# Moving the second layer's first projections into the first layer's feed-forward, pairing the early maximum tiles, and taking the up product off VectorE

## The reference, cut to what matters

```python
# layer 0 feed-forward, weights of three values
hidden = silu(xn @ wu.T) * (xn @ wg.T);  out = hidden @ wd.T
# layer 1 attention, 16 heads of 16
q, k = rope(xn @ q_w.T + q_b), rope(xn @ k_w.T + k_b);  v = xn @ v_w.T + v_b
probs = softmax(q @ k.T * 0.25);  out = (probs @ v) @ out_w.T + out_b
# layer 1 feed-forward (fwht: Walsh-Hadamard transform)
h = fwht(xn * SU_ug) / 64
h = silu(h @ W_gate.T * wsg) * (h @ W_up.T * wsu)
out = (fwht(h * SU_dp) / 64) @ W_down.T * wsd
```

## Time and profile before

| | us |
|---|---|
| median of 3 runs | 798.71 (797.28 to 798.75) |
| the profiled execution | 799.5 |
| its span, first to last instruction | 797.7 |
| TensorE busy | 722.2 (91%) |
| VectorE busy | 568.9 (71%) |
| ScalarE busy | 416.1 (52%) |
| GpSimd busy | 247.7 (31%) |

### The profile page before, as it was taken

How to read it: one execution, slowest core, us unless ns; L and a number is a source line. 1 busy time by engine, 2 the same in 40 slices (tenths; PEclk the granted TensorE clock), 3 DMA queues, 4 the chain that set the end, 5 groups by cost and what they waited for, 6 DMA issues and landing times.

```text
span 797.7 us, 10977 instructions
## 1 busy us (share of the span) xinstructions
PE 722.2 (91%) x4190; PEld 446.2 (56%) x4190; DVE 568.9 (71%) x922; ACT 416.1 (52%) x547; POOL 247.7 (31%) x241
## 2 busy tenths in 40 slices
PE   3678798969697989899999999999999999999997
PEld 3467687957466878656656656533333433333344
DVE  4887666675365664898898998688888468888016
ACT  2532323345254433132122122799999899999983
POOL 0156855333224444231121021112124313412520
PEclk9988999999799999999999999999999999999999
DMA  6145101000101246443311110234444424433321
GB/s 241 54 148 185 51 0 53 1 1 1 53 1 53 80 139 208 154 154 111 106 54 54 54 49 6 70 127 153 124 146 134 140 81 134 152 115 101 114 61 54
DMA packets 25703, 74.13 MB, mean 93 GB/s; under 512 B 4604, under 2 KB 5980, under 8 KB 24692
## 3 DMA queue, kind: packets, MB, share of 16 engines
q1 hardware_dynamic: 21124, 65.37, 24.6%
q0 software_dynamic: 3808, 7.60, 3.3%
q10 hardware_dynamic: 720, 0.48, 0.2%
HBM read 54.54 MB, written 23.06 MB: 97 GB/s over the span
## 4 chain that ended last, share of the span: by engine, by line
PE 66%; DVE 16%; issue 7%; ACT 6%; POOL 2%; DMA 1%; SPq 0%; DVEq 0%; ACTq 0%; POOLq 0%
PE PS L718 20%; PE PS L959 15%; PE PS L945 11%; PE PS L724 9%; PE PS L928 6%; DVE mx L1238 4%; PE PS L918 4%; DMA stg<-in_wa 1%; ACT P L1412 1%; DVE XD L1046 1%; PE PS L798 1%; DVE sg L1177 1%; DVE sg L1169 1%; DVE XL L1053 1%; ACT sg L1378 1%
## 5 line engine op out<-in xcount | busy, mean ns | idle before, releaser
L1412 ACT ACTIVATE P<-PS 128x1024 f32<-128x1024 f32 x256 | 248.8, 1023 | 26.7 <-PE PS L945 26.3
L1245 DVE TENSOR_REDUCE mx<-PS 128x1 f32<-128x512 f32 x288 | 181.9, 682 | 31.1 <-PE PS L928 29.7
L1490 POOL TENSOR_TENSOR hl<-sg,hh 128x512 fp32r<-128x512 f32 x64 | 83.1, 1299 | 222.6 <-ACT hh L1385 222.6
L1238 DVE TENSOR_REDUCE mx<-PS 128x2 f32<-128x1024 f32 x112 | 132.2, 1218 | 15.0 <-PE PS L918 14.5
L959 PE MATMUL PS<-P,VV 128*32 128x512 f32 x1024 | 136.4, 605 | 0.1
L945 PE MATMUL PS<-QS,KS 64*128 64x512 f32 x512 | 116.1, 457 | 1.2 <-ACT P L1412 0.9
L945 PEld LDWEIGHTS PS<-QS,KS 64*128 64x128 f32 x512 | 48.1, 183 | 122.9 <-ACT P L1412 112.3
L1385 ACT ACTIVATE hh<-sg 128x512 fp32r<-128x512 f32 x64 | 40.4, 631 | 135.6 <-DVE sg L1180 83.9
L928 PE MATMUL PS<-KM,QM 64*128 64x512 f32 x288 | 77.5, 396 | 0.0
L1380 ACT ACTIVATE sg<-PS,cols 128x512 f32<-128x512 f32 x32 | 22.0, 689 | 82.7 <-PE PS L718 82.7
L918 PE MATMUL PS<-KM,QM 64*128 64x512 f32 x224 | 51.5, 484 | 9.7 <-DVE mx L1238 7.1
(11 more groups left out here) (199 smaller groups left out, 1353.0 us busy)
## 6 DMA issues: line engine op xcount, KB each, us to landing
QM<-scr_q SPq DMA_DIRECT2D x16, 512.0 KB, 4.4
KM<-scr_k SPq DMA_DIRECT2D x16, 512.0 KB, 5.4
QS<-scr_q SPq DMA_DIRECT2D x16, 512.0 KB, 4.4
KS<-scr_k SPq DMA_DIRECT2D x16, 512.0 KB, 5.3
scr_q<-spl SPq DMA_DIRECT2D x24, 256.0 KB, 3.4
scr_k<-spl SPq DMA_DIRECT2D x24, 256.0 KB, 3.1
scr_o<-OE POOLq DMA_DIRECT2D x14, 256.0 KB, 2.6
stg<-in_tern SPq DMA_DIRECT2D x3, 1024.0 KB, 4.8
```

The lines of the kernel that those rows point to most:

```text
L1238: e.tensor_reduce(mx[p % 2][:, :, qt, half], PS[:, b:b + 2, :], AX.X, ALU.max).then_inc(q["mx"], 2)
L1245: e.tensor_reduce(mx[p % 2][:, h, qt, half:half + 1], bank[b], AX.X, ALU.max).then_inc(q["mx"], 1)
L1412: e.activation(P[s % 4][:, half * 1024:(half + 1) * 1024], PS[:, b:b + 2, :].rearrange("p b n -> p (b n)"), ACT.Exp).then_inc(q["ex"], 1)
L1490: e.tensor_tensor(hl[f % 4][:, :], sg[f % 3][:, :], r32(hh[f % 4][:, :]), ALU.subtract).then_inc(q["hl"], 1)
```

## The change

- Four of the eight projections (chunks 0 and 1, queries and keys) with their rotations, splits and writes move into the end of `side0`. Their rotation and split buffers are a set of their own (`rots[0]`, `spls[0]`), in the space of the weights' staging. The tables `COS` and `SIN` load at the start of layer 0's last chunk in the list, and need only the norms of chunks 0 and 1 done; chunk 2 and 3's norms get another buffer. `load_m(0)` and `load_m(1)` are put before the end of layer 0.
- `RATE0` goes from 0.8 to 0.9; what is left of `side0` is no longer emptied before layer 1 but runs on in front of `side1`.
- Early tiles are put in twos (`two`), and beside the last projections each two comes with a value block. The rates are 0.9 for the first 32 steps and then 0.64 twos a step (before: 1.15 for 22 steps, then 1.62 tiles a step). `EARLY` goes from 112 to 106. The row of maxima takes a bank of `pf`, one tile later.
- In layer 1 the up block is read out of PSUM by ScalarE (`us = up * wsu`), the product `sg * us` is done by GpSimd, and the high part (`hidden`) follows behind the next gate in ScalarE's queue, the low part with it on GpSimd. `us` lies in the same space as `hh`. The up block's bank is free after ScalarE's copy.

```diff
-EARLY, MOST = 112, 3
+EARLY, MOST = 106, 3
 
 PROJECT = (56, 112, 120)
 FIRST = 12
-RATE0 = 0.8
-RATE1 = 1.15
-RATE2 = 1.62
+RATE0 = 0.9
+RATE1 = 0.9
+RATE2 = 0.64
...
         for m in range(8):
             bg = pf.next()
             put("gate", layer, c, m, bg)
+            if layer and m:
+                put("hidden", c, m - 1)
             yield
             put("up", layer, c, m, pf.next())
             yield
...
         for m in (5, 6, 7):
             put("down", layer, c, m)
+            if layer and m == 5:
+                put("hidden", c, 7)
             yield
         put("ffn_end", layer, c)
...
+    def qk(c, n, between, count):
+        put("qk", c, n, ps.next(), ps.next())
+        yield
+        for _ in range(count):
+            between()
+            yield
+        put("qk_split", c, n)
...
+        for c in (0, 1):
+            for n in range(2):
+                yield from qk(c, n, lambda: None, 4)
+        put("load_m", 0)
+        put("load_m", 1)
...
+                if (layer, c, k) == (0, 3, 0):
                     put("load_cs")
...
-    for _ in sd0:
-        pass
...
-            if u == 2 and p > 0:
-                rows(p - 1, ring)
+            if u == 3 and p > 0:
+                rows(p - 1, pf)
...
-        def qk(c, n, between, count):
-            put("qk", c, n, ps.next(), ps.next())
-            yield
-            for _ in range(count):
-                between()
-                yield
-            put("qk_split", c, n)
-
         def v():
-            put("v", next(tts), ps.next())
-
-        def early():
+            tt = next(tts, None)
+            if tt is not None:
+                put("v", tt, ps.next())
+
+        def two():
             tile(ps)
-
+            tile(ps)
+
+        def two_and_v():
+            two()
+            v()
+
+        yield
+        yield
         for i in range(4):
             put("ones_v", i)
-        for c in (0, 1):
-            for n in range(2):
-                yield from qk(c, n, v, 3)
-        put("load_m", 0)
-        put("load_m", 1)
+        yield
         yield from qk(2, 0, v, 4)
-        yield from qk(2, 1, early, 4)
+        yield from qk(2, 1, two_and_v, 4)
         for n in range(2):
-            yield from qk(3, n, early, 5)
+            yield from qk(3, n, two_and_v, 4)
         while len([o for o in order if o[0] == "max"]) < EARLY:
-            early()
+            two()
             yield
 
-    sd1 = side1()
+    sd1 = chain(sd0, side1())
     main1 = main(1)
-    weave(islice(main1, 22), sd1, RATE1)
+    weave(islice(main1, 32), sd1, RATE1)
     weave(main1, sd1, RATE2)
     for _ in sd1:
         pass
...
+        us = [sb(f"us{i}", (156, 158, 160, 76)[i], [128, 512]) for i in range(4)]
...
-        XD = [sb(f"XD{i}", 16 + 4 * i, [128, 4, 256]) for i in range(2)]
+        XD = [sb(f"XD{i}", (16, 20, 198)[i], [128, 4, 256]) for i in range(3)]
...
-        rot = [sb(f"rot{i}", 84 + 2 * i, [128, 512]) for i in range(4)]
-        spl = [sb(f"spl{i}", 92 + 2 * i, [128, 512], F32R) for i in range(4)]
+        rots = [[sb(f"rot{b}{i}", (190, 84)[b] + 2 * i, [128, 512]) for i in range(4)] for b in range(2)]
+        spls = [[sb(f"spl{b}{i}", (174, 92)[b] + 2 * i, [128, 512], F32R) for i in range(4)] for b in range(2)]
...
-                e.wait_ge(q["lnb"], 14)
+                e.wait_ge(q["lnb"], 12)
...
             def load_m(p):
                 if p == 0:
-                    e.wait_ge(q["lnl"], 16)
+                    e.wait_ge(q["d"], 32)
                     e.wait_ge(d["pad"], 32)
...
                     e.wait_ge(q["bx"], 8)
+                    e.wait_ge(q["lnl"], 16)
...
                 sums(bank[b], wide(TG, None, m * 128, c) if layer == 0 else wide(UGH, UGL, m * 128, c)).then_inc(q["u"], 1)
-                freed[b] = q["h"], f + 1
+                freed[b] = (q["h"], f + 1) if layer == 0 else (q["ue"], f - 31)
...
-                if n == 6:
-                    e.wait_ge(q["lnb"], 10)
                 if n == 7:
-                    e.wait_ge(q["pd"], 4)
+                    e.wait_ge(q["lnb"], 14)
...
             def up(layer, c, m, b):
-                f = 32 * layer + 8 * c + m
+                if layer:
+                    return
+                f = 8 * c + m
                 s = sg[f % 3]
                 e.wait_ge(q["u"], f + 1)
-                if layer == 0:
-                    e.wait_ge(q["v1"], f + 1)
-                    e.tensor_tensor(s[:, :], s[:, :], bank[b], ALU.mult).then_inc(q["h"], 1)
-                else:
-                    e.wait_ge(q["t"], f + 1)
-                    e.scalar_tensor_tensor(s[:, :], bank[b], col("wsu", m), s[:, :], ALU.mult, ALU.mult).then_inc(q["h"], 1)
+                e.wait_ge(q["v1"], f + 1)
+                e.tensor_tensor(s[:, :], s[:, :], bank[b], ALU.mult).then_inc(q["h"], 1)
...
                 if i == 0:
                     e.wait_ge(d["cs"], 32)
+                    e.wait_ge(q["pd"], 4)
+                if i == 4:
                     e.wait_ge(q["d"], 32)
...
             def up(layer, c, m, b):
                 f = 32 * layer + 8 * c + m
+                if layer == 0:
+                    e.wait_ge(q["h"], f + 1)
+                    e.activation(hh[f % 4][:, :], sg[f % 3][:, :], ACT.Copy).then_inc(q["hh"], 1)
+                else:
+                    e.wait_ge(q["u"], f + 1)
+                    e.activation(us[f % 4][:, :], bank[b], ACT.Copy, scale=col("wsu", m)).then_inc(q["ue"], 1)
+
+            def hidden(c, m):
+                f = 32 + 8 * c + m
                 e.wait_ge(q["h"], f + 1)
                 e.activation(hh[f % 4][:, :], sg[f % 3][:, :], ACT.Copy).then_inc(q["hh"], 1)
...
+                    if i == 0:
+                        e.wait_ge(q["pu"], 4)
+                    else:
                         e.wait_ge(d[f"sp{2 * m}"], 32 * i)
...
+            def low_part(f):
+                e.wait_ge(q["hh"], f + 1)
+                e.tensor_tensor(hl[f % 4][:, :], sg[f % 3][:, :], r32(hh[f % 4][:, :]), ALU.subtract).then_inc(q["hl"], 1)
+
             def up(layer, c, m, b):
                 f = 32 * layer + 8 * c + m
-                e.wait_ge(q["hh"], f + 1)
-                e.tensor_tensor(hl[f % 4][:, :], sg[f % 3][:, :], r32(hh[f % 4][:, :]), ALU.subtract).then_inc(q["hl"], 1)
+                if layer == 0:
+                    low_part(f)
+                else:
+                    s = sg[f % 3]
+                    e.wait_ge(q["ue"], f - 31)
+                    e.tensor_tensor(s[:, :], s[:, :], us[f % 4][:, :], ALU.mult).then_inc(q["h"], 1)
+
+            def hidden(c, m):
+                low_part(32 + 8 * c + m)
...
+                    for j in range(4):
+                        e.wait_ge(d[f"sp{j}"], (128, 64)[j % 2])
```

15 lines of the change are left out of this document (9 added, 6 removed).

## The result

The changed kernel takes 812.19 us (median of 4 runs, 811.05 to 812.99) against 798.73 for the kernel before (4 runs): a ratio of 1.0171, 95% interval 1.0154 to 1.0189. I had predicted 786. The profiled execution of after took 811.97 us, its span is 810.2.

A forecast was written before the change was run, and what follows sets the result against it. It took VectorE as the bound in layer two's chunks 1 to 3 and TensorE in the last stage. Terms -19.3 - 0.8 + 6 + 0.7 = -13.4 against 799.5 gave 786.1, said as 786, range 775 to 797.

The forecast's parts named there:

- Chunks 1 to 3: Layer two's later chunks: fewer tiles, all in twos, and a relieved VectorE take 153.0 us for 172.3, -19.3.
- The up chain: Layer two's copy, product, high and low part: 4.3 us, hidden in a 6.4 us period, cost 0 to 0.5.
- Layer two's first chunk: Fewer projections and value blocks but more tiles: 75.0 us for 75.8, -0.8, bounds -6 and +5.
- 14 value blocks, 20 tiles in twos, 64.7: Layer two's first chunk: TensorE's work after the change, with 4 projections, 64.7 us, before waits of 11.3 less 1.
- Layer one: Four projections add 11.1 us, 6 of the stall and half clock go, packing adds 1: +6, bounds 0 and +18.
- the attention is packed denser, +1: Layer one: 0.9 side pieces for 0.8 beside the feed-forward cost 1 us.
- So 39.5: Layer one's last chunk: 31.9 us of TensorE work plus waits of 2.5, 2.7 and 2.3; before it took 39.2.
- Last stage: Exponentials and remaining maxima: six tiles become 12 more halves, filling four steps, +0.7 us.
- Slower than before: Rival: each projection moved into layer one exposes rotation and split, +34 there, -20 in layer two: 812; chance 0.07.
- The first layer pays: Rival: VectorE bounds layer one's last chunk, waits double, half clock follows, +14 for +6: 794; chance 0.13.
- The bursts are absorbed: Rival: waits of 3 in layer two's chunks 1 to 3, layer one's stall gone, +1 there: 776; chance 0.15.
- It does not do what it says: Rival: the up chain sets layer two's pace and TensorE waits for low parts: no change, 799; chance 0.05.

The follow-up runs named there:

- before_up: The kernel before with only layer two's up product moved, as a copy on ScalarE and a product on GpSimd: 803.5 us.
- vfirst_upback: The changed kernel with the value block ahead of the two tiles and layer two's up product on VectorE again: 798.1 us.
- after_v_first: The changed kernel with the value block put ahead of the two tiles, not behind them: 799.5 us.
- before_rate09: The kernel before with one number changed, 0.9 side pieces for each piece of layer one's feed-forward, for 0.8: 800.0 us.
- vfirst_staged: The changed kernel with the value block first and layer one's side pieces at 0.8 for chunks 0 and 1, 1.15 behind them: 791.8 us.
- light_rot: As light_sum, with the rotation's two sine products of each of these projections over 16 columns too: 790.8 us.
- vfirst_norm: The changed kernel with the value block first and chunk 2's layernorm six pieces earlier in layer one's last chunk: 797.1 us.
- before_twos_up: The kernel before with early tiles in twos and the up product on ScalarE and GpSimd, projections staying in layer two: 791.1 us.
- light_sum: The changed kernel with the value block first and GpSimd's two sums of each layer-one projection over 16 columns for 512: 796.6 us.

## Why the prediction was wrong, point by point

The profiled executions differ by +12.5 us (811.97 to 799.5), where I had -13.4: 25.9 too low. Layer one makes 15.4 of it (+21.4 for +6), layer two's first chunk 6.2 (+5.4 for -0.8), chunks 1 to 3 5.4 (-13.9 for -19.3), and the work ahead of layer one took 0.9 less.

By experiment the loss is made up so: twos -2.5 (795.1), the up product on top -4.0 (791.1), the four projections with the denser side pieces +8.4 (799.5), and the value block behind the tiles +12.7 (812.2). The base of this sum is the 797.6 of the kernel before on the chip of the first two; on others it had 797.8 and 798.7, so each term is good to about 1 us.

**What bounds the kernel (wrong).** I read the earlier trace rows as VectorE being the bound in chunks 1 to 3. before_up shows 5 us less of VectorE's work in each of chunks 2 and 3 and 0.4 us of gain; with tiles in twos the same relief gave 1.5 to 1.7. The earlier trace rows counts weight loads that wait for a reduction, 21.8 us, but most of that lies under running products: the products themselves waited 9.7 there, in the same view of before:

```profile
PE PS L918 <- DVE mx L1238: 7.1, 13, 1.4
PE PS L934 <- DVE mx L1238: 2.2, 3, 0.9
PE PS L718 <- DVE mx L1238: 0.4, 1, 0.4
```

In the changed kernel the gain in these chunks came from fewer tiles and from pairs: with the up product back on VectorE they take 154.7 us (vfirst_upback), with it moved 156.2 (after_v_first), and most of that difference is the lower clock in chunk 1.

**Chunks 1 to 3 (right in kind, 5.4 short).** 158.2 for 153.0. TensorE's waits there are 11.4 us, near the 12.1 that I had (10.8 and 1.3), but made up otherwise: 17 short ones behind tiles take 4.9, some 0.3 each, where I had 18 of 0.6; one of 3.8 stands behind the splits at 374.76, two of 1.2 are value blocks', and 0.3 is a low part. So a burst was priced twice too high, and that the sum of the waits fits is luck. What is short is the work: chunk 1 ran at a granted clock of 0.94, and in chunks 2 and 3, at 1.00, my prices give 90.6 us for the pieces and the trace 3.4 of waits, together 94.0, where 96.4 were measured. The up chain was as forecast: TensorE waited for a low part once, 0.3 us.

**Layer two's first chunk (wrong).** The step that failed is the working "14 value blocks, 20 tiles in twos, 64.7" with waits for rotations only. I counted the products and not whose bank each took. Without the bank waits it took 71.9, 3.1 below my 75.0; with them 81.3. The order of the pieces has them, `max`, `max`, `v`, each with its bank. The 75.0 would have come near by luck: the waits other than these were 4.1 us in after_v_first where I had 10.3, and the work took 67.8 where I had 64.7.

**Layer one (wrong).** The sum was 11.1 for the projections' products, -6 for the stall and +1 for the packing. The steps that failed are two. The four projections cost 21.7 us against before_rate09, so 10.6 beyond their products, for which the sum has nothing. And -6 + 1 came out as -0.3 (194.45 for 194.75). Both are differences of single executions, and before_rate09's was a quick one, so they are good to a few microseconds; the medians have before_rate09 2.2 us above before on the same chip. As for the packing, "the attention is packed denser, +1" cost 12.9 in chunk 0 of before_rate09, 14.3 in that of after, and undone behind projections (vfirst_staged) it gives 7.4 back. I had named a term and given it a number with no row behind it; the rows that would have shown it are GpSimd's fold of 4.6 us, a butterfly of 2.5 and a low part, behind which the attention's `ek` is queued. before_rate09 gets this back in chunks 1 to 3 (2.2, 3.2 and 7.8 us): there the stall's 6.2 + 4.5 us are gone, and the last chunk has no preparations left; in after, three projections took up that room.

"So 39.5" for the last chunk: 47.1. The waits were 11.5 us where I had 7.5, since the norm's was 7.94 and not 2.7, and the granted clock fell to 0.89, which I had not charged. A sign of being wrong that I had named, a last chunk beyond 45 us, came. In the trace VectorE waits 1.22 for ScalarE's high part of the split (a wait I had left out), then has two splits in 1.96 (1.7 by my price), the rotation in 2.7 and the norm in 3.28 in front of TensorE's transposes. light_rot, with GpSimd's sums and half of VectorE's rotation left out, takes 5.7 us off the chunk and so supports that this length is what matters; vfirst_norm shows that the norm's place does not. Bounds of "0 and +18" for the layer were too narrow on the upper side, since the stall and the rotations were bounded and the packing was not.

**Last stage (right).** +0.5 for +0.7 from the first scores on. Executions with the same pieces there took 293.2 (after) to 295.4 (before_twos_up) in this stretch, so the agreement is closer than the spread.

**Rivals.** "Slower than before", 812, has the right total, with 7 in 100 given to it, by two errors that cancel, which is luck. It had +34 in layer one, of which 23 beyond the projections' products; measured is +21.4, and 10.6 beyond the products (21.7 - 11.1, against before_rate09), which is past the 9 us that it had named as its sign. It had -20 in layer two, which is what after_v_first shows (248.0 to 228.1); in after the value block's waits leave -8.5. "The first layer pays" had the mechanism of the last chunk, longer waits with half clock behind them, but +14 for the layer and nothing of the packing. "The bursts are absorbed" adds up to 772 to 773 by its own terms, not 776; its short waits came (4.9 us), its +1 in layer one did not. "It does not do what it says" is refuted: the up chain never set the pace.

## What to carry to other kernels

Follow each piece's bank as well as its product: a piece put behind one that has just filled the ring waits for that one whatever the engines' load, and swapping two lines was worth more here (12.7 us) than any part of the change. An engine at 90% busy is the bound only if taking work from it shortens the stretch; here 5 us of relief gave 0.4 with lone tiles and 1.6 with pairs, while in another chunk an engine at 73% with an in-order queue passed its microseconds on nearly one for one. Try a change's parts alone before giving the whole up: two of its three parts, with two places moved, made the kernel 1.8% faster.

## What the runs showed of the hardware

- Ten executions of after_v_first lie at 796.4 to 798.0 us (five) and 800.9 to 802.1 (five), with mean granted clocks of 0.959 to 0.972 and 0.955 to 0.966; before_rate09 and vfirst_norm, which share its packing of layer one, leave a like gap (796.1 to 799.1 and 800.8 to 803.5), while vfirst_upback and light_sum, which share it too, spread over 3.2 and 2.7 us without one. In chunk 1 of layer two the same pieces with the same 4.5 us of waits took 59.8 us at a clock of 0.94 (after_v_first) and 58.5 at 0.97 (light_rot, vfirst_staged). What decides between them isn't settled here.
- Two VectorE splits that read SBUF twice took 1.28 us alone and, beside GpSimd's low part and product, 3.00 (before_up) and 3.06 (after), while reductions out of PSUM in the same stretches kept 1.2.
- Where TensorE had waited 4.6 and 7.9 us, the granted clock of the next 15 and 19 us was 0.82 (before_up from 357, after from 261); ten waits of up to 1.2 us in layer two's first chunk of after left it at 0.98 over the chunk.
